# Two-phase attention kernel: the second feed-forward product in float32r parts made by GpSimd, with a new order in one kind of window and an earlier input split

## The reference, cut to what matters

```python
for l in range(2):
    h = shift_token(x)
    q, k, v = split(h @ wqkv)
    q, k = rotary(l2norm(q) * qs, l2norm(k) * ksc)
    x = x + local_attention(q, k, v) @ wo
    h = layernorm(shift_token(x)) * lg + lb
    a, g = split(h @ w1 + b1)
    x = x + (a * gelu(g)) @ w2 + b2      # the last product is the one that changes
```

## Time and profile before

| what | us |
|---|---|
| median of 3 runs (lowest to highest) | 5561.13 (5558.59 to 5565.03) |
| the profiled execution | 5557.89 |
| its span | 5555.8 |
| TensorE busy | 5271.0 (95%) |
| VectorE busy | 4168.2 (75%) |
| ScalarE busy | 3509.1 (63%) |
| GpSimd busy | 1259.2 (23%) |

### The profile page before, as it was taken

One profiled execution on the slowest core, in us unless ns is written; L12 is line 12 of the kernel. 1 busy time (PEld: TensorE's weight loads), 2 busy tenths in 40 slices (PEclk: granted clock), 3 DMA queues, 4 the chain that ended last, 5 costly groups with the idle time before them and its releaser, 6 DMA issues.

```text
span 5555.8 us, 150327 instructions
## 1 busy us (share of the span) xinstructions
PE 5271.0 (95%) x59592; PEld 2996.7 (54%) x59592; DVE 4168.2 (75%) x10819; ACT 3509.1 (63%) x7119; POOL 1259.2 (23%) x2489
## 2 busy tenths in 40 slices
PE   8999999999999999999789999999999999999997
PEld 3444444444444444544356666666666666666664
DVE  6888878888887888878567777777776777777774
ACT  4676667666666766767556566565565656656664
POOL 2222222222222222222212112111122121221211
PEclk9999999999999999999899999999999999999999
DMA  3333333233333333323110000000000000000000
GB/s 71 56 56 66 54 62 61 50 71 56 64 55 54 69 54 69 54 50 68 44 43 12 16 9 16 16 9 16 16 26 26 20 16 20 24 16 20 16 20 20
DMA packets 128829, 216.97 MB, mean 39 GB/s; under 512 B 40064, under 2 KB 40192, under 8 KB 127360
## 3 DMA queue, kind: packets, MB, share of 16 engines
q1 hardware_dynamic: 128128, 207.35, 18.4%
HBM read 46.78 MB, written 25.17 MB: 13 GB/s over the span
## 4 chain that ended last, share of the span: by engine, by line
PE 64%; ACT 15%; DVE 10%; issue 7%; POOL 4%; DMA 0%; POOLq 0%; ACTq 0%; SPq 0%; DVEq 0%
PE ps L617 23%; PE ps L746 14%; PE ps L1108 6%; PE ps L869 4%; ACT pt L1327 3%; PE ps L970 3%; PE ps L951 3%; PE ps L943 2%; ACT sm L1461 2%; DVE sm L1922 2%; ACT gates L1559 1%; PE ps L1049 1%; PE ps L1045 1%; PE ps L1046 1%; PE ps L927 1%
## 5 line engine op out<-in xcount | busy, mean ns | idle before, releaser
L1327 ACT ACTIVATE pt<-ps 128x1024 f32<-128x1024 f32 (+7 forms) x2048 | 1237.4, 654 | 620.1 <-PE ps L617 464.4
L746 PE MATMUL ps<-pt,va 128*32 128x512 f32 (+3 forms) x3072 | 1226.3, 487 | 22.3 <-POOL pt L2224 22.2
L746 PE MATMUL ps<-pt,ones 128*32 128x512 f32 (+3 forms) x6144 | 1236.3, 488 | 0.0
L746 PE MATMUL ps<-pt,vs 128*32 128x512 f32 (+3 forms) x3072 | 1230.0, 488 | 0.0
L1748 DVE CUSTOM_DVE_ANT_0 junk<-ps,causal 128x128 bf16<-128x128 f32 (+3 forms) x2048 | 978.1, 488 | 307.5 <-PE ps L617 291.7
L617 PE MATMUL ps<-kt,qt 96*32 96x512 bf16 (+3 forms) x12288 | 1017.4, 328 | 35.5 <-DVE mc L1748 16.3
L2224 POOL TENSOR_SCALAR_AFFINE_SELECT pt<-pt 128x256 f32<-128x256 f32 x1024 | 465.8, 455 | 1937.8 <-ACT pt L1327 1936.3
L617 PE MATMUL ps<-qt,kt 98*32 98x512 bf16 (+3 forms) x12288 | 836.6, 328 | 22.8 <-ACT pt L1327 22.0
L1752 DVE TENSOR_REDUCE mc<-ps 128x1 f32<-128x512 f32 x1024 | 706.4, 690 | 155.2 <-PE ps L617 124.5
L617 PEld LDWEIGHTS ps<-kt,qt 96*32 96x32 bf16 x12288 | 335.7, 94 | 578.4 <-DVE mc L1752 224.8
L1461 ACT ACTIVATE sm<-sm,mxw 128x256 f32<-128x256 f32 (+1 forms) x1024 | 494.0, 486 | 150.1 <-DVE mxw L1922 149.7
(11 more groups left out here) (170 smaller groups left out, 10221.6 us busy)
## 6 DMA issues: line engine op xcount, KB each, us to landing
qt<-part SPq DMA_DIRECT2D x768, 64.0 KB, 2.4
kt<-part SPq DMA_DIRECT2D x768, 64.0 KB, 2.5
ya<-wy SPq DMA_DIRECT2D x128, 128.0 KB, 2.3
yb<-wy SPq DMA_DIRECT2D x128, 128.0 KB, 2.3
xs<-between_phases SPq DMA_DIRECT2D x32, 512.0 KB, 3.8
xt<-in_x SPq DMA_DIRECT2D x16, 512.0 KB, 6.2
between_phases<-z SPq DMA_DIRECT2D x16, 512.0 KB, 2.8
between_phases<-xo SPq DMA_DIRECT2D x16, 512.0 KB, 2.7
```

The costliest lines, as they stand in the source:

```text
L746: mmi = pe.matmul(ps[32 * q:32 * q + 32, 4 + half, lo - half * 512:hi - half * 512], w, probs(kb)[:, i, lo - first(kb):hi - first(kb)], st ...
L1327: act.activation(probs(kb)[:, i, kb * P - first(kb):1024 - first(kb)], ps[:, 2 * i:2 * i + 2, :].rearrange("p a q -> p (a q)")[:, kb * P:1 ...
```

## The change

`hh` is no longer a tensor of its own: `gated` writes into `gates` in place, GpSimd makes the high part `hhh` (a cast) and then the low part `hhl` (a subtraction, over `gates`), block by block (`inner_low`), and TensorE does three float32r products for each float32 one. `w2` is split once a layer, by ScalarE and GpSimd (`split_w2`). The input split gets three buffers instead of two, and stands at the start of a window's work on GpSimd in kinds 0 to 2, and behind the combine in kind 3. In kind 0, keys go ahead of the first transpose of probabilities, squares and norms go forward, the rotation is done between the normalisings, and the final add goes behind the residuals. On GpSimd the sum over channels goes ahead of the final one, also in the tail.

```diff
-                    pe.wait_ge(hh_done, done(m * HB + 6))
+                    pe.wait_ge(w2l_done, done(m // (2 * nb) + 1))
+                    pe.wait_ge(hh_done, done(m * HB + 5))
...
-                    mmi = pe.matmul(ps[:, fbank(m, 19 + oc), :], w2[rows, j, oc * P:(oc + 1) * P], hh[rows, j, :],
-                                    start=j == 0, stop=j == HB - 1)
+                    if oc == 0:
+                        pe.wait_ge(hhl_done, done(m * HB + j + 1))
+                    pe.matmul(out, w2h[rows, j, cols], hhh[rows, j, :], start=j == 0, stop=False)
+                    pe.matmul(out, w2l[rows, j, cols], hhh[rows, j, :], start=False, stop=False)
+                    mmi = pe.matmul(out, w2h[rows, j, cols], hhl[rows, j, :], start=False, stop=j == HB - 1)
@@ TensorE, kind 0 @@
-                    transpose_p(W, 0)
                     keys(W + 1, 0)
                     keys(W + 1, 1)
+                    transpose_p(W, 0)
@@ ScalarE @@
+                act.activation(w2h[:, :, :], w2[:, :, :], ACT.Copy).then_inc(w2h_done, 1)
@@ ScalarE, kind 0 @@
                     exps(W, 1)
+                    squares(W + 1)
                     place_p(W, 0)
                     exps(W, 2)
-                    exps(W, 3)
-                    squares(W + 1)
+                    inverse_norms(W + 1)
                     values(W)
                     place_p(W, 1)
-                    inverse_norms(W + 1)
+                    exps(W, 3)
@@ GpSimd @@
+            def inner_low(m, j):
+                rows = slice(0, P if j < HB - 1 else HLAST)
+                pool.wait_ge(hh_done, done(m * HB + j + 1))
+                pool.wait_ge(w2_full, done(2 * m))
+                pool.tensor_copy(hhh[rows, j, :], gb_[rows, j, :]).then_inc(hhh_done, 1)
+                pool.wait_ge(hhh_done, done(m * HB + j + 1))
+                pool.tensor_tensor(hhl[rows, j, :], gb_[rows, j, :], hhh[rows, j, :], ALU.subtract).then_inc(hhl_done, 1)
+            def split_w2(l):
+                pool.wait_ge(w2h_done, done(l + 1))
+                pool.tensor_tensor(w2l[:, :, :], w2[:, :, :], w2h[:, :, :], ALU.subtract).then_inc(w2l_done, 1)
...
+                if W % 4 < 3:
+                    split_x(W + 2)
                 if m >= 0 and W % 4 == 1:
                     inputs_low(m)
                 if W + 1 < LAST:
                     combine(W + 1)
-                split_x(W + 2)
-                if W == nb * WIN - 2:
-                    split_wqkv(1, 0)
-                    split_wqkv(1, 1)
+                if W % 4 == 3:
+                    split_x(W + 2)
...
+                if m >= 0 and W % 4 == 2:
+                    inner_low(m, 0)
+                    pool.wait_ge(rot_done, done(W + 2))
+                    for j in range(1, HB):
+                        inner_low(m, j)
+                if W == nb * WIN - 2:
+                    split_wqkv(1, 0)
+                    split_wqkv(1, 1)
@@ GpSimd, the tail @@
             m = half_of(LAST)
+            sum_channels(m)
             final_channels(m - 1)
-            sum_channels(m)
             final_sum_squares(m - 1)
```

More of the change, by code:

```diff
@@ L273, in program @@
         w2 = sb("w2", [P, HB, 256], F32)
+        w2l = low_of("w2", "w2l", [P, HB, 256])
+        w2h = sb("w2h", [P, HB, 256], F32R)
         lnp = sb("lnp", [P, 2, 2], F32)
@@ L278, in program @@
         gb_ = sb("gates", [P, HB, 512], F32)
-        glast = sb("glast", [HLAST, 512], F32)
-        hh = sb("hh", [P, HB, 512], F32)
+        hhl = low_of("gates", "hhl", [P, HB, 512])
+        hhh = sb("hhh", [P, HB, 512], F32R)
+        glast = nc.alloc_sbuf_tensor_at("glast", [HLAST, 512], F32, offset=places["hhh"] + (HB - 1) * 2048)
         xo = sb("xo", [P, 2, 512], F32)
@@ L402, in program @@
         w2_full = sem("w2_full")
+        hhh_done = sem("hhh_done")
+        hhl_done = sem("hhl_done")
+        w2h_done = sem("w2h_done")
+        w2l_done = sem("w2l_done")
         xo_done = sem("xo_done")
@@ L1540, in gate_out @@
                     act.wait_ge(b1_done, done(m // (2 * nb) + 1))
-                    act.wait_ge(hh_done, done(m * HB))
+                    act.wait_ge(w2_full, done(2 * m))
                 act.wait_ge(g_full, done(m * HB + j + 1))
@@ L1610, in attend @@
                     final_squares(m - 1)
+                    if W % (nb * WIN) == 5:
+                        split_w2(W // (nb * WIN))
                     if m < 0:
@@ L2042, in attend @@
                     largest(W, 3)
-                    final_add(m - 1)
                     normalise(W, 1)
+                    norms(W + 1)
+                    rotate_own(W + 1)
                     normalise(W, 2)
+                    rotate_other(W + 1)
                     normalise(W, 3)
@@ L2054, in attend @@
                     residual(m, 1)
+                    final_add(m - 1)
                     centre(m)
@@ L2288, in split_x @@
                     pool.wait_ge(xs_ready[w // 4], sent(lb + 1))
-                if W >= 2:
-                    pool.wait_ge(v_full, done(W - 1))
+                if W >= 3:
+                    pool.wait_ge(v_full, done(W - 2))
                 for kc in range(2):
                     at = w * P + 1 - kc
-                    i = pool.tensor_copy(xh[:, W % 2, kc, :], xs[:, kc, at:at + P])
+                    i = pool.tensor_copy(xh[:, W % 3, kc, :], xs[:, kc, at:at + P])
                 i.then_inc(xh_done, 1)
@@ L2329, in _ @@
                     final_sum_squares(m - 1)
+                if W % (nb * WIN) == 5:
+                    split_w2(W // (nb * WIN))
+                if m >= 0 and W % 4 == 2:
[6 more added lines that the diff above has]
+                    split_wqkv(1, 1)
+                if W == nb * WIN - 1:
+                    split_wqkv(1, 2)
             m = half_of(LAST)
+            sum_channels(m)
             final_channels(m - 1)
-            sum_channels(m)
             final_sum_squares(m - 1)
@@ L2335, in _ @@
             inputs_low(m)
+            for j in range(HB):
+                inner_low(m, j)
             final_channels(m)
```

29 lines of the change are left out of this document (13 added, 16 removed).

## The result

| | before | after |
|---|---|---|
| median (lowest to highest), us | 5560.9 (5558.6 to 5565.0) | 5602.0 (5599.7 to 5603.9) |
| ratio, 95% interval | 1 | 1.0073 [1.0061, 1.0085] |
| span of the profiled execution | 5555.8 | 5600.3 |
| mean granted clock of TensorE | 0.991 | 0.984 |

What follows compares the result with a forecast made beforehand. TensorE, busy 95% of the span, was taken to bound the kernel. Kind 3 at 0, kind 0 at -5 and once-only costs at +10 gave +5 us: 5563 profiled, 5566 as median, range 5526 to 5602.

Steps and rivals of the forecast that it cites:

- case A: Whole kernel: VectorE's waits eat what TensorE saves; 5566 us, own range 5554 to 5578, chance 0.40.
- rival D: Kind 3: normalise(0), (1) and (2) each wait for a subtraction, 2.0 in all; +30, 5596 us, chance 0.27.
- kind 3 and what follows it: Windows with W % 4 = 3: TensorE's saving of 1.05 a half cancelled by a rotation 1.05 late, net 0.
- kind 0, layer one: Windows with W % 4 = 0, first layer: reordered work saves 0.7 for two halves, -5 us over eight pairs.
- kind 0, layer two, narrow / wide: Second layer, W % 4 = 0: final add delays GpSimd's sum; narrow windows lose 0.6, wide gain 0.6, together 0.
- w2 split: Done twice, on ScalarE and GpSimd: delays exps 1.1 and normalise(0) 2.1, +3.2 each, +6.4.
- W = 4: Windows W = 4 and 68: norms no longer wait for the bias product, -1.5 each.
- The change of places on GpSimd and VectorE: Kind 3: GpSimd and VectorE take turns by whole instructions; normalise(0) 0.3 late, normalise(1) and the rotation 1.05 late.
- the 0.6 behind it pays that back: Kind 3: the two product blocks behind line 918 shrink from 2.00 to 1.4, offsetting that line coming 0.6 later.
- once only: One-time costs: W = 62 low parts +3, w2 splits, W = 4 and 68, tail; together +10, bounds +3 to +18.
- C: Whole kernel: the cheaper product counts in full, 2.3 a half in kind 3, 70 us; 5496 us, chance 0.03.
- B: Kind 3: GpSimd and VectorE meet little, giving back 1.05 a half, 33 us; 5534 us, chance 0.30.

Runs made afterwards that it cites:

- run 2: Changed kernel with the float32 second product put back, leaving the new order of kind 0, input split and final add: 5561.3 us, 1.0006 of before.
- run 4: Changed kernel with seven more products of 512 columns on TensorE in kind 3, in the time it stands: 5589.7 us, 1.0057 of before.
- run 3: Changed kernel without GpSimd's subtractions in inner_low, casts only, the third product part reading the high part again: 5541.9 us, 0.9972 of before.
- run 7: Changed kernel without GpSimd's wait for the rotation ahead of the second cast and subtraction pair: 5616.3 us, 1.0105 of before.
- run 5: Changed kernel with exps(3) moved on ScalarE in kind 3 to behind the squares, ahead of inverse_norms: 5531.7 us, 0.9954 of before.
- run 11: Kernel of run 8 with TensorE's blocks (1, 2) and (1, 3) of kind 3 left out: 5522.5 us, 0.9936 of before.
- run 8: Run 5 plus final add at the start of kind 0, projection's low parts between those of W = 62, tail in old order: 5512.0 us, 0.9917 of before.
- run 6: Kernel before the change with only exps(3) moved early on ScalarE in kind 3: 5561.5 us, 1.0003 of before.
- run 1: Changed kernel with the old kind 0 order, input split, final add and tail put back, leaving the product change: 5603.3 us, 1.0087 of before.
- run 10: Kernel of run 8 with TensorE's blocks (1, 0) and (1, 1) of kind 3 left out: 5518.3 us, 0.9923 of before.

## Why the prediction was right or wrong

The forecast of 5566 was 36 low; the range, to 5602, holds the time of 5601.95 by 0.05 us, and that is luck: the two largest parts of the loss, the clock's 19.6 and the 8.4 ahead of the second phase, are in no term of the sum. The likeliest case A (its own range ended at 5578) did not come true as priced, and rival D had the time (5596) with a mechanism that did not happen. Term by term, from the profiled executions:

| term | forecast | measured |
|---|---|---|
| kind 3 and what follows it, a half | -1.05 + 1.05 = 0 | +0.60 - 0.33 = +0.27 |
| kind 0, layer one (a pair of halves) | -0.7 | -0.66 |
| kind 0, layer two, narrow / wide | +0.6 / -0.6 | +0.54 / -0.63 |
| windows 8 to 59 and 72 to 126, without clock | -5 | +1.8 |
| the same, clock | none | +19.6 |
| W = 0 to 7 (w2 split +3.2, W = 4 -1.5) | +1.7 | +4.7 |
| W = 60 to 71 (+3, +3.2, -1.5) | +4.7 | +6.7 |
| behind the last window | +3.4 | +3.2 |
| ahead of the second phase | 0 | +8.4 |

The last six rows add up to 44.4 measured, against 44.5 between the spans. Kind 0's are from run 2, and "without clock" is from run 4. The other rows hold low clock too, more than before: 7.3 us at 0.5 in W = 0 to 7, 3.4 in W = 60 to 71, 4.9 behind the last window, 20.0 ahead of the second phase. At the 3.1 for 6.8 of W = 80 this is an estimate of at most 3.3, 1.6, 2.2 and 9.1 (less where TensorE stands anyway).

**Right.** *The change of places on GpSimd and VectorE.* The cast is 0.61 and the pair 2.0, as estimated. Normalise(0), (1) and (2) take 0.94, 1.58 and 0.69: 1.14 more, of which 1.02 reaches the rotation (1.05 forecast), and run 3 gives 0.99 back. A VectorE instruction with two inputs in SBUF and a GpSimd instruction wait for each other as wholes; those with an input in PSUM were not held. The Trainium skill (GPSIMD Engine Reference, 8. Key points) names VectorE instructions with two SBUF inputs as contending with GpSimd. Runs 3 and 7 agree: 0.99 a half given back without the subtractions, and normalise at 1.53 in kind 2 without the hold. *Line 925 late by the delay less the slack*: 1.02 - 0.45 = 0.57, +0.60 measured. *Kind 0*, in both layers and both widths. *The tail.*

**Wrong: "the 0.6 behind it pays that back".** From line 925 to 934 is 2.17, 2.44 before: 0.27. Two blocks of three parts cost 1.4 by spacing, but they took 1.76, from 5091.44 to 5093.20: next to a change of operand sizes two starts lie 0.31 to 0.34 apart and not 0.23 (5091.44 to 5091.75, 5092.31 to 5092.65). With what kind 0 gives back in all, 0.33 instead of 0.6, that is the path's share of the miss, 0.27 a half, 8 us.

**Wrong: a step that was missing.** I priced a stand of TensorE at its length, nothing more; it appears in my text only as "some 2 us" that the profile would show, and for the tail. It also lowers the granted clock behind it, which costs 19.6 in the steady windows of the profiled execution, nearly half of the loss. Run 4 (stand filled: gone), runs 3 and 5 (stand shortened: gone) and run 11 (stand made: back in part) show it. The trace of before had the sign: its second phase has no low stretch between 2840 and 5500 but the three at the border of the layers, and the first of these begins 0.3 behind the stand of 2.93.

**Wrong in size: once only.** W = 63 is +7.3, not +3: TensorE stood 10.22 for the low parts,

```profile
L876 PE MATMUL ps<-wqh,xh 128*128 128x512 f32 x768 | 348.7, 454 | 11.2 <-POOL wql L2233 10.2
```

They start 10.9 behind the eviction and not 9.7, which holds the queries 7.3 longer than before and not 5 to 6. One subtraction ahead of them took 2.74: it met two VectorE instructions with two SBUF inputs, which are no normalise and stood in no step of mine,

```profile
4093.46 0.72 DVE L2033 TENSOR_TENSOR gates<-gates,glast 42x512 f32<-42x512 f32 x1
4094.11 1.21 DVE L1879 TENSOR_TENSOR tab<-tab,scl 128x1024 f32<-128x1024 f32 x1
...
4093.72 2.74 POOL L2286 TENSOR_TENSOR hhl<-gates,hhh 128x512 fp32r<-128x512 f32 x1
```

Normalise(0) and (1) there take 1.25 and 0.91 instead of 0.82 and 2.61, but the products behind the stand run at 0.5 for 6.0 us instead of 3.4, and of the 1.9 that I gave back nothing is left in the window. In run 8 the two stands there are 2.92 and 0.98.

**Right, and hidden by the clock: the split of w2 and W = 4.** Where its window holds no low clock the split costs 2.97 (W = 70 in the changed kernel and in run 5, W = 6 in run 11), against 3.2 forecast; W = 6 of the changed kernel is +4.30 with 3.4 us at 0.5. W = 4 was +2.2 and not -1.5, but it holds 6.6 us more at 0.5 than before, worth some 3.0; in run 6, which changes nothing in that window, it is +3.95 with 8.4 us more. So most of that miss is the clock's; why the clock lies low there in every other run stays open.

**Two slips of reckoning.** The lower bound of kind 0, -14, is some -18 by its own terms (0.7 x 8 and (1.15 + 0.4) x 8); nothing hung on it. And one sign was drawn wrongly: from one line 925 to the next, case A has kind 3 longer by 0.6 and not "as before", since the two blocks behind line 925 belong to the next window. Measured is +0.60.

**Not the change's, or not shown to be.** Before the second phase begins, the profiled execution is 8.4 behind, with 59 us of low clock against 39. No instruction there is changed. Run 6, whose buffers lie as before, is 3.9 behind at that point, runs 2 and 3 2.6, run 4 7.2, and all the others between: the execution of before has the shortest first phase of the thirteen and the changed kernel's the longest. I take it as the spread of that phase; whether the changed kernel's lies high every time was not tested.

**The rivals.** C was rightly given next to nothing. B (33 us faster, engines meet little) is what run 3 shows as a kernel without subtractions: 15 faster. What I missed in all four is that the rotation had 1.35 to give: VectorE stood for exps(3), which ScalarE could have had done by 5083, while it idled 1.59 for the norms. "Nothing in that chain takes up slack" was true of the order as written, and one line made it untrue (run 5).

## What to carry to other kernels

When work is taken from the busiest engine, follow the chain that it waits for next, with every idle gap on it: the gain here (28 us) came only after one line of another engine's order had shortened that chain by 1.6. A new stand can be dearer than its length when it is one piece before busy work, so look at the granted clock, window by window; filler in the stand is a cheap test. Keep elementwise work of GpSimd away from VectorE instructions with two SBUF inputs on the path: each meeting costs up to one whole instruction.

## What the runs showed of the hardware

- Stretches of 3.4 or 6.8 us at 0.5 (1.2 GHz) came behind some stands before line 925 of 1.66 (8 of 27 in the changed kernel, 10 of 27 in run 1) and of 1.5 (4 of 27 in run 11), the border aside. None came behind two of 0.78 and 0.54 (run 10), one of 0.99 (run 3) or, in run 7, stands of 0.8 to 1.4; the one of 1.74 there had one.
- The taking of turns goes both ways and is by the instruction: subtraction 1.29 alone, 1.6 beside a normalise and 2.74 beside two VectorE instructions of 0.72 and 1.21 at the border; cast 0.61 alone, up to 1.54; normalise 0.69 alone, 0.94 and 1.58; the sum 1.27 alone, 2.18.
- A GpSimd subtraction of 42 partitions takes as long as one of 128 (1.28 and 1.29, both 512 columns).
